# Cross attention on one core: packed Gram rows, their diagonal corrected apart, and each tile's projection finished bank by bank

## The reference

```python
text_p  = x @ W_text + b_text                 # 512 -> 512
audio_p = ctx @ W_audio + b_audio             # 384 -> 512
Q = layer_norm(text_p, g1, beta1)
K = layer_norm(audio_p, g2, beta2)
alpha = softmax(Q @ K.T / sqrt(512))          # over 77 keys
h = (alpha @ audio_p) @ W_out + b_out
out = layer_norm(h + x, g_out, beta_out)
```

## Time and profile before

| what | us |
|---|---|
| median of 3 runs | 277.99 |
| lowest and highest run | 277.51, 280.63 |
| span of the profiled execution | 275.9 |
| its own time beside the span | not listed apart; the median is 2.1 above the span |
| busy: TensorE products, VectorE, GpSimd, ScalarE | 265.3, 230.5, 203.3, 202.3 |

### The profile page before, as it was taken

One profiled execution on the slowest core, in us unless ns is written; L12 is line 12 of the kernel. 1 busy time (PEld: TensorE's weight loads), 2 busy tenths in 40 slices (PEclk: granted clock), 3 DMA queues, 4 the chain that ended last, 5 costly groups with the idle time before them and its releaser, 6 DMA issues.

```text
span 275.9 us, 5994 instructions
## 1 busy us (share of the span) xinstructions
PE 265.3 (96%) x1705; PEld 236.7 (86%) x1705; DVE 230.5 (84%) x716; ACT 202.3 (73%) x509; POOL 203.3 (74%) x223
## 2 busy tenths in 40 slices
PE   7999999999999999999999999999999999999980
PEld 6789689899999999999999999999999999999830
DVE  3767899788888888888888888888888888888895
ACT  4584392357888888888888888888888888888881
POOL 5071400114699999999999999999999999999985
PEclk9999999999999999999999999999999999999997
DMA  6818894422244444444444444444444444444116
GB/s 210 317 59 308 289 318 135 128 74 77 77 154 153 156 152 153 154 152 153 152 153 152 152 152 153 153 152 152 152 152 154 153 152 152 152 153 150 79 77 266
DMA packets 21056, 44.03 MB, mean 160 GB/s; under 512 B 2114, under 2 KB 4750, under 8 KB 21034
## 3 DMA queue, kind: packets, MB, share of 16 engines
q1 hardware_dynamic: 20410, 42.74, 45.8%
q10 hardware_dynamic: 624, 1.06, 1.2%
HBM read 21.19 MB, written 16.78 MB: 138 GB/s over the span
## 4 chain that ended last, share of the span: by engine, by line
PE 85%; DVE 5%; ACT 3%; POOL 3%; issue 1%; ACTq 1%; POOLq 0%; DVEq 0%
PE psY L1268 43%; PE psO L1280 10%; PE psT L1193 10%; PE psY L1258 7%; PE psE L1243 3%; PE psE L1244 2%; PE psY L1098 2%; PE psT L1131 1%; PE psY L1162 1%; PE psT L1162 1%; POOL zs L460 1%; POOL zs L464 1%; POOL rstd L452 1%; PE psY L1131 1%; ACTq L488 1%
## 5 line engine op out<-in xcount | busy, mean ns | idle before, releaser
L1268 PE MATMUL psY<-proj_hi,x_hi 128*128 128x464 f32 (+3 forms) x256 | 85.9, 335 | 0.0
L1268 PE MATMUL psY<-proj_hi,x_lo 128*128 128x464 f32 (+3 forms) x256 | 83.1, 325 | 0.0
L1268 PE MATMUL psY<-proj_lo,x_hi 128*128 128x464 f32 (+3 forms) x256 | 82.9, 324 | 0.0
L429 POOL TENSOR_TENSOR zs<-zs,shift 128x512 f32<-128x512 f32 x55 | 71.0, 1291 | 4.3
L423 POOL TENSOR_TENSOR zs<-zs,gain 128x512 f32<-128x512 f32 x55 | 71.0, 1291 | 1.0 <-ACT zs L616 1.0
L435 POOL TENSOR_TENSOR rstd<-stat_eps,neg_half 128x4 f32<-128x4 f32 x30 | 30.5, 1017 | 41.8 <-DVE stat_eps L921 41.8
L605 ACT ACTIVATE waste_act<-hid,sc 128x512 bf16<-128x512 f32 x60 | 43.1, 718 | 9.9 <-DVE hid L929 9.9
L1268 PEld LDWEIGHTS psY<-proj_hi,x_lo 128*128 128x128 f32 x256 | 48.4, 189 | 1.4
L1268 PEld LDWEIGHTS psY<-proj_hi,x_hi 128*128 128x128 f32 x256 | 48.6, 190 | 0.8
L1268 PEld LDWEIGHTS psY<-proj_lo,x_hi 128*128 128x128 f32 x256 | 48.6, 190 | 0.7
L574 ACT ACTIVATE x_hi<-psT 128x512 fp32r<-128x512 f32 x64 | 38.1, 596 | 13.9 <-PE psT L1193 13.9
(11 more groups left out here) (230 smaller groups left out, 487.8 us busy)
## 6 DMA issues: line engine op xcount, KB each, us to landing
xs<-in_x_dram SPq DMA_DIRECT2D x64, 256.0 KB, 3.0
out_dram<-zs SPq DMA_DIRECT2D x29, 512.0 KB, 3.9
out_dram<-zs SPq DMA_DIRECT2D x6, 256.0 KB, 2.0
xs<-in_L_xattn_W_text_dram SPq DMA_DIRECT2D x4, 256.0 KB, 3.2
xs<-in_L_xattn_W_out_dram SPq DMA_DIRECT2D x2, 512.0 KB, 5.2
wa<-in_L_xattn_W_audio_dram SPq DMA_DIRECT2D x1, 768.0 KB, 5.9
proj_hi<-proj_hi SPq DMA_DIRECT2D x1, 768.0 KB, 9.1
proj_lo<-proj_lo SPq DMA_DIRECT2D x1, 768.0 KB, 11.1
```

What stands on the lines that cost most here:

```text
L429: nc.gpsimd.tensor_tensor(zs[:, q, t, :], zs[:, q, t, :], shift[:], ALU.add).then_inc(out_ready, 1)
L1268: last = nc.tensor.matmul(psY[:, t, to:to + n0], part[:, par, t, k * P:(k + 1) * P], w[:, q, at:at + n0], start=(n == 0), stop=(n == len(P ...
```

## The change

1. **Layout.** One matrix `proj` takes the place of `proj_hi` and `proj_lo`. It has four block rows of 672 columns (ROW_W), in two halves of 336 (HALF = 80 + 256), one for each bank. The left half has 80 further columns (root, 77 low score parts, filling, low `lin`) and Gram columns 0 to 255, the right one Gram columns 256 to 511 and 80 further ones (`lin`, root, 77 high score parts, NX).
2. **Gram rows.** The high part of the doubled upper triangle stays in the upper columns; the low part is turned (transposed) and put in the free lower columns of the same rows. The blocks on the diagonal hold the halved upper triangle beside the turned low one (GpSimd, `triangle`, with `mask`; `turn`, ten transposes; ScalarE, four copies from TURNED; GpSimd adds).
3. **Exact diagonal.** The diagonal of G is found apart (`gram_square`, four squares with sums on ScalarE), nearly all of it is kept in G, and the square root of the rest (`root`, GpSimd, a power of 0.5) is a further column. `less_root` takes root times root out of each Gram row by a product over three partitions; the form adds it again, since `sc` now stands in x's row in SBUF, one column behind x.
4. **Projection.** Fourteen products a tile: `x_hi` by the left half (four of 336 columns), `x_lo` by the left Gram columns (256 and 128), then `x_hi` by the right half (four of 336), `x_lo` by the right half (three of 336, one of 208). 4288 columns. The probability transposes stand behind the first right product.
5. **The form** reads `sc` as an operand and waits for `sc_ready`, once a tile.
6. **Moves.** `t_lo(0)` and `t_hi(0)` come behind the audio work; Gram row 3 has twelve products of 128 columns; the four Gram copies of SyncE come behind the x loads of the fourth batch.

```diff
-    WIDTH = [SW + D] + [D - k * P + SW for k in range(1, KD)]
+    HALF = SW + D // 2
+    ROW_W = 2 * HALF
...
-        proj_hi = sb("proj_hi", [P, B, COLS], F32R)
-        proj_lo = sb("proj_lo", [P, B, COLS], F32R)
+        proj = sb("proj", [P, B, KD, ROW_W], F32R)
...
-        sc = sb("sc", [P, B, T, SC])
+        sc = xs_rows[:, :, :, SC_AT:SC_AT + SC]
...
 scores_and_quad:
                 nc.vector.tensor_tensor(sc[:, q, t, :], psY[:, t, at:at + SC], sc_part[:, t, :], ALU.add).then_inc(sc_ready, 1)
+                wait_if_positive(dve, sc_ready, T, i, T * (b - 1) + t + 1)
                 nc.vector.tensor_tensor_reduce(out=waste_dve[:, t, 0:QUAD_W], in0=psY[:, t, QUAD_AT:QUAD_AT + QUAD_W],
...
 project:
-                for n, (part, w) in enumerate(parts3(x_hi, x_lo, proj_hi, proj_lo)):
-                    last = nc.tensor.matmul(psY[:, t, B_AT:512], part[:, par, t, 0:P], w[:, q, 0:SW + P],
-                                            start=(n == 0), stop=(n == 2))
+                for k in range(KD):
+                    high(k, 0)
+                wait_if_positive(pe, x_lo_ready, T, i, T * (b - 1) + t + 1)
+                for k in range(2):
+                    last = nc.tensor.matmul(psY[:, t, B_AT + SW + k * P:512], x_lo[:, par, t, k * P:(k + 1) * P],
+                                            proj[:, q, k, SW + k * P:HALF], start=False, stop=(k == 1))
                 last.then_inc(projB_psum, 1)
-                for n, (part, w, k) in enumerate(PASSES):
-                    if n == passes_before and between is not None:
+                for k in range(KD):
+                    if k == before and between is not None:
                         between(b, i)
+                    high(k, 1)
+                for k in range(KD):
+                    skip = P if k == KD - 1 else 0
+                    last = nc.tensor.matmul(psY[:, t, 512 + skip:512 + HALF], x_lo[:, par, t, k * P:(k + 1) * P],
+                                            proj[:, q, k, HALF + skip:ROW_W], start=False, stop=(k == KD - 1))
                 last.then_inc(proj_psum, 1)
...
 the end:
-            project(0, END, 1, transpose_prob, 6)
+            project(0, END, 1, transpose_prob)
...
 tensor engine, preparation:
+            pe.wait_ge(root_cols_ready, 6)
+            for n, bank in ((0, ROOT_BANK[1]), (1, ROOT_BANK[0])):
+                for k in range(KD):
+                    last = nc.tensor.transpose(bank[0:3, k * P:(k + 1) * P], f32(root_cols[:, k, 3 * n:3 * n + 3]), ident[:])
+                last.then_inc(root_psum, 1)
             gram(1)
+            less_root(0)
+            less_root(1)
...
             gram(2)
-            last_gram()
+            less_root(2)
+            gram(3)
+            less_root(3)
...
             last.then_inc(kvar_psum, 1)
+            for j in range(KD):
+                turn(j)
             pe.wait_ge(g_lo, 2)
             values_product(1)
...
 GpSimd, preparation:
+            def triangle(k):
+                pool.wait_ge(g_lo, k + 1)
+                nc.gpsimd.tensor_tensor(rest[k][:, 0:P], f32(rest[k][:, 0:P]), mask[:], ALU.mult).then_inc(mask_ready, 1)
+                at = SW + k * P
+                nc.gpsimd.tensor_tensor(upper[:, k, :], f32(proj[:, 0, k, at:at + P]), mask[:], ALU.mult).then_inc(upper_ready, 1)
```

More of the change, by code:

```diff
@@ L128, in cross_attention @@
         bo_rows = sb("bo_rows", [P, H])
+        mask = sb("mask", [P, P])
+        half = sb("half", [P, KD])
+        gram_diag = sb("gram_diag", [P, KD])
+        gram_kept = sb("gram_kept", [P, KD], F32R)
+        gram_left = sb("gram_left", [P, KD])
+        root = sb("root", [P, KD])
+        root_cols = sb("root_cols", [P, KD, 6], F32R)
         cd_cols = sb("cd_cols", [P, KH, 2])
@@ L173, in cross_attention @@
         assert KH == B
+        spare_hi = x_hi[:, 1].rearrange("p t d -> p (t d)")
+        spare_lo = x_lo[:, 1].rearrange("p t d -> p (t d)")
+        rest = [spare_lo[:, 0:D], spare_lo[:, D:2 * D - P], spare_hi[:, 0:2 * P], spare_hi[:, 2 * P:3 * P]]
+        upper = spare_hi[:, 3 * P:7 * P].rearrange("p (k n) -> p k n", k=KD)
+        root_rows = x_hi[0:3, 0]
         val_a, val_b = wo_hi, wo_lo
@@ L300, in copy_gram @@
             def copy_gram(k):
-                at, n = Y_AT[k], D - k * P
-                for buf, made in ((proj_hi, g_hi), (proj_lo, g_lo)):
-                    sp.wait_ge(made, k + 1)
-                    one = f32(buf[:, 0:1, at:at + n])
-                    sp.dma_start(f32(buf[:, 1:B, at:at + n]), one.to_broadcast([P, B - 1, n])).then_inc(t_copied, 16)
+                sp.wait_ge(gram_ready, k + 1)
+                one = f32(proj[:, 0:1, k, SW:SW + D])
+                sp.dma_start(f32(proj[:, 1:B, k, SW:SW + D]), one.to_broadcast([P, B - 1, D])).then_inc(t_copied, 16)
             def body(b, i, live):
@@ L799, in _ @@
                     linear(k)
+                if k == 0:
+                    root_parts()
+            dve.wait_ge(root_psum, 1)
+            nc.vector.tensor_copy(root_rows[:, 1, :], ROOT_BANK[1][0:3, :]).then_inc(root_rows_ready, 1)
+            linear(2)
+            t_lo(0)
             t_lo(1)
-            linear(2)
             def lo_part(b, i, t):
@@ L817, in _ @@
             link(nc.vector.memset(kvar[:], 1.0))
-            last_gram_sum()
+            for k in range(2, KD):
+                t_lo(k)
             dve.wait_ge(kvar_psum, 1)
@@ L822, in _ @@
             last.then_inc(kvar_ready, 1)
-            for k in range(2, KD):
-                t_lo(k)
             linear(KD - 1)
@@ L937, in shifted_logits @@
                 for t in range(T):
-                    nc.vector.scalar_tensor_tensor(logits[:, b % 2, t, :], sc[:, q, t, 0:S], rstd[:, b, t:t + 1],
+                    nc.vector.scalar_tensor_tensor(logits[:, b % 2, t, :], sc[:, q, t, 1:1 + S], rstd[:, b, t:t + 1],
                                                    score_d[:, q, :], ALU.mult, ALU.add).then_inc(logits_ready, 1)
@@ L1033, in last_logits @@
                 dve.wait_ge(sc_ready, T * LAST + t + 1)
-                nc.vector.scalar_tensor_tensor(logits[:, LAST % 2, t, :], sc[:, q, t, 0:S], rstd[:, r, t:t + 1], score_d[:, q, :],
+                nc.vector.scalar_tensor_tensor(logits[:, LAST % 2, t, :], sc[:, q, t, 1:1 + S], rstd[:, r, t:t + 1], score_d[:, q, :],
                                                ALU.mult, ALU.add).then_inc(logits_ready, 1)
@@ L1115, in _ @@
                 last.then_inc(cxT_psum, 1)
-            def last_gram():
-                k = KD - 1
-                for h in range(KH):
-                    last = nc.tensor.matmul(W_BANK[k][:, 0:2 * P].rearrange("p (a n) -> p a n", a=2), wtT_hi[:, h, k * P:D],
-                                            wtT[:, :, h, k * P:D], start=(h == 0), stop=(h == KH - 1))
-                last.then_inc(g_psum, 1)
             def gram(k):
@@ L1154, in _, with turn @@
             gram(2)
-            last_gram()
+            less_root(2)
+            gram(3)
+            less_root(3)
+            def turn(j):
+                pe.wait_ge(mask_ready, j + 1)
+                for k in range(j + 1):
+                    last = nc.tensor.transpose(TURNED[j][:, k * P:(k + 1) * P], f32(rest[k][:, (j - k) * P:(j - k + 1) * P]), ident[:])
+                if j > 0:
+                    last.then_inc(turned_psum, 1)
             def values_product(n):
@@ L1233, in _ @@
             constant(0, C_BANK)
-            pe.wait_ge(lin_lo_ready, KD)
-            PASSES = [(a, w, k) for k in (1, 0, 2, 3) for a, w in parts3(x_hi, x_lo, proj_hi, proj_lo)]
+            pe.wait_ge(lin_lo_ready, 3)
+            pe.wait_ge(gram_ready, KD)
             def transpose_prob(b, i):
```

207 lines of the change are left out of this document (120 added, 87 removed).

## The result

| kernel | median, us | runs | lowest to highest |
|---|---|---|---|
| before, beside it | 279.31 | 4 | 277.51 to 281.94 |
| changed | 283.35 | 4 | 281.64 to 285.74 |

The ratio is 1.018, with a 95% interval of 1.013 to 1.024: the changed kernel is slower. I had forecast 278.8 with a range from 272.5 to 282.5. The same kernel, run once more beside the experiments, gave 283.25 (4 runs, 281.04 to 284.69) against 278.36 (13 runs), again 1.018 [1.009 to 1.027].

The account below looks back on a forecast made before the run. A loop of VectorE and the tensor engine waiting for each other was taken as the bound. 275.9 + 3.4 (preparation) - 2.6 (steps) - 0.4 (first) + 0.4 (last) = 276.7, plus 2.1 to the median: 278.8 us, range 272.5 to 282.5.

Parts of the forecast that it names:

- The failed step: Preparation: the root and its parts on VectorE and GpSimd were taken as hidden under the audio products, at no cost.
- The added work of the tensor engine: Preparation: the tensor engine works without a gap, so added transposes and products delay everything by 3.4 us.
- the products that take the root out: Preparation, tensor engine: four products of 512 to 128 columns, at 0.119 per 256, add 0.65 us.
- the last Gram row: Preparation, tensor engine: twelve products of 128 columns, 1.32 us, in place of four in 0.48, add 0.84 us.
- rival (c): Preparation: GpSimd's eight masked 128x128 products hold the turning if 0.87 us each or more; 281.7 or 283.3 us, chance 0.15.
- The steady step: Repeated step: a loop of VectorE and the tensor engine still bounds, falling from 6.855 to 6.77 us.
- The tensor engine's part of the loop: Steady step: fewer product columns behind the probability transposes shorten this part by 0.27 us.
- The wait in tile 1: Steady step, VectorE: the form waiting for sc costs 0.12 us in the loop, bounds nothing to 0.17.
- The second: Steady step: the other tile's wait for sc, partly covered by ScalarE's rounding, costs 0.06 us.
- The waits: Signs in steady step: VectorE below 0.4, tensor engine for parts near 0.5, GpSimd before rstd near 0.25, sc to form 0.28.
- Rival (a): Steady step: the tensor engine bounds and the step falls until GpSimd holds at 6.52; 270.9 us, chance 0.11.
- Rival (b): Steady step: the added waits on VectorE are free, so the step is 6.585; 273.0 us, chance 0.17.

Follow-up runs that it names:

- Experiment 1: Changed kernel, but GpSimd waits for the root columns before its four wo_lo subtractions: 277.87 us, ratio 1.001.
- experiment 8: Changed kernel with GpSimd's four wo_lo subtractions of 512 columns cut into eight of 256: 279.27 us, one run.
- experiment 4: Kernel before, with the probability transposes behind six products of the right bank instead of three: 281.59 us, ratio 1.011.
- experiment 5: Kernel before, with only the wait of the quadratic form for sc added: 281.82 us, one run, step 6.975.
- experiment 9: Changed kernel, but tile 0's form reads 514 columns without root part or wait; tile 1 keeps both: 280.06 us, one run, step 6.693.
- experiment 2: Changed kernel, with the form of both tiles reading 514 columns, without the root column and without the wait for sc: 280.24 us, step 6.564.
- experiment 3: Changed kernel, with the probability transposes behind the third high right product instead of the first: 277.85 us, ratio 0.999.
- experiment 6: Changed kernel, with GpSimd's wo_lo after the root columns and the probability transposes behind the third high right product: 274.79 us, ratio 0.987.
- experiment 7: Changed kernel, with GpSimd's wo_lo after the root columns and the probability transposes behind the second high right product: 273.19 us, ratio 0.979.
- 6 and 7 with less of GpSimd's work: Kernels of experiment 6 and experiment 7, with GpSimd's output shift added on 256 instead of 512 columns for each step's second tile: 273.94 and 273.41 us.

## Why the prediction was wrong

**The failed step** is the sentence of the preparation "Hidden: ... the root and its parts on VectorE and GpSimd (under the audio products)". I looked at how much work it is, six instructions on 128 x 4 numbers, and not at who runs beside it. GpSimd's `wo_lo` stands in the earlier trace rows, 6.07 us from 15.84 on, exactly there. Experiment 1 gives the columns back at 0.17 each, and experiment 8 shows that four of the six each wait out one GpSimd instruction.

The first audio product itself starts between 12.50 and 16.39 us, also in executions of kernels that do not differ up to there, as the loads come (16.39 and 15.97 have a stretch at clock 0.50 ahead of it too). So the preparation is best counted from that product (us):

| profiled execution | first audio product | from it to the root transposes | from it to the first projection |
|---|---|---|---|
| kernel before; experiments 4 and 5 | 12.50; 12.68, 12.87 | | 32.04 to 32.07 |
| changed, clock full behind the root columns (again; experiment 9) | 13.50; 12.57 | 8.99 | 39.10 |
| changed, clock 0.50 there (first profile; experiments 2 and 3) | 12.71; 13.56, 15.97 | 8.99 | 40.43 to 40.59 |
| root first (experiments 1, 6, 7, and 6 and 7 with less of GpSimd's work) | 12.87 to 16.39 | 6.22 | 36.33 to 36.35 |
| halved pieces (experiment 8) | 13.94 | 6.84 | 36.99 |

The wait for the root columns costs 39.10 - 36.35 = 2.75 us, where I had priced it at nothing, and the lower clock behind it 40.59 - 39.10 = 1.5 more in the first profile. Without the wait alone, 283.35 - 2.75 = 280.6 would have stood inside my range.

**The added work of the tensor engine** was sized low: 3.4 forecast, 36.35 - 32.07 = 4.3 measured once the wait is gone. Its terms, from the profile of experiment 7, where they stand undisturbed (the first row is of the kernel before):

```profile
12.50 4.83 PE L1098 MATMUL psY<-cxT,wa 128*128 128x308 f32 x18
...
12.99 4.83 PE L1154 MATMUL psY<-cxT,wa 128*128 128x308 f32 x18
...
20.00 2.34 PE L1179 MATMUL psY<-wtT 128*128 128x384 f32 x12
22.27 0.49 PE L1184 MATMUL psT<-x_hi 3*128 3x512 f32 x1
...
25.93 1.55 PE L1179 MATMUL psO<-wtT 128*128 128x128 f32 x12
27.41 0.32 PE L1184 MATMUL psO<-x_hi 3*128 3x128 f32 x1
...
31.18 0.55 PE L1221 MATMUL psY<-ident,x_lo 128*128 128x128 f32 x3
...
32.24 0.48 PE L1230 MATMUL psY<-wo_hi,vT_hi 128*128 128x512 f32 x1
```

The eight root transposes 0.79 (0.88 forecast), with 0.2 between the audio products and them; the products that take the root out 0.59 for the first two and 0.3 each for the others, 1.2 together (0.65), each 0.1 to 0.2 above what I took for its columns (that the change of shape costs it is a guess, not tried); the last Gram row 27.41 - 25.93 = 1.48 against 0.48, so 1.0 (0.84); the ten turns 1.06 (1.10). These add up to the 4.3 within 0.1. The 0.5 between the first two rows is not part of it: by the table, it is the loads of that execution.

**GpSimd's masked products** (rival (c)) take 0.46 each (a row of experiment 7 below), near my 0.38 and far from the 0.87 from which they decide. The turns follow the key variances without a wait. The side was right, slower, and the mechanism was not: it was GpSimd's large instructions that held VectorE, not its small ones that held the tensor engine.

```profile
24.68 0.46 POOL L428 TENSOR_TENSOR x_hi<-proj,mask 128x128 fp32r<-128x128 f32 x1
```

**The steady step.** Forecast 6.77, measured 6.69. The tensor engine's part of the loop fell as forecast: from the first product behind the transposes to the mix it is 138.44 - 137.34 = 1.10 us, where it was 152.56 - 151.18 = 1.38 (rows below and the earlier trace rows): 0.28 less, 0.27 forecast. The wait in tile 1 cost the forecast 0.12 (experiments 2 and 5). The second was put at 0.06 and is free (experiments 5 and 9): ScalarE's branch covers it in full. 6.855 - 0.27 + 0.12 = 6.705. Behind the first projection the kernel saved 4.7 us, where I had 2.6 in the steps, 0.4 in the first one and 0.4 lost at the end, so 2.6 net.

```profile
137.34 0.71 PE L1328 MATMUL psY<-proj,x_hi 128*128 128x336 f32 x3
...
138.44 0.41 PE L1358 MATMUL psO<-wo_hi,parts_t 128*128 128x512 f32 x1
```

The mix in the kernel before:

```profile
152.56 0.41 PE L1280 MATMUL psO<-wo_hi,parts_t 128*128 128x512 f32 x1
```

**The waits** came out as said: VectorE 0.3 (below 0.4), the tensor engine 0.4 (near 0.5), `rstd` 0.18 (0.25), `sc` to form 0.27 (0.28).

**Rival (a)**, the tensor engine as the bound, is false for this kernel, whose chain goes by VectorE more than by the tensor engine (the page's shares below), and true for the one with late transposes, at 6.34 of its own work, not the 6.25 that I gave it: its work fell by 6.76 - 6.34 = 0.42 a step, where I had 0.55. **Rival (b)**, waits that are free, is refuted by experiments 2 and 5. The Trainium skill, "VectorE: DVE Perf Modes", section "The DRAIN you can't avoid", says that semaphores between vector instructions cost nothing extra. Here one costs 0.12 us, because the two instructions overlap when nothing holds the second.

```profile
DVE 47%; PE 31%; issue 15%; ACT 4%; POOL 1%; ACTq 1%; DVEq 0%; POOLq 0%
```

The Trainium skill, "SBUF — State Buffer", section "🔬 SBUF: two separate sides", would have caught the failed step. VectorE and GpSimd share one pair of ports, as an exclusive lock held for the whole instruction, and the other engine blocks fully; it names VectorE's two-port modes and its instructions with two SBUF inputs. The trace agrees, in both kinds: the casts and scalings (one input) and the subtraction (two). What is 0.17 us alone is 1.2 beside 128 x 512 subtractions and 0.67 beside 128 x 256 ones.

**What stays open.** Why the changed kernel had the lower clock in half of its runs. In the first 260 us of the fourteen profiled executions the tensor engine stood idle for 1.75 us or more seven times: five times for the root columns (2.61 us), once for the load of the context (2.00, experiment 3) and once for a part of the text weights (1.75, experiment 1). The granted clock fell to 0.50 near the end of five of these seven, three of them waits for the root columns, and nowhere else in that stretch. So the idle time bears on it. But it isn't the whole cause: the clock stayed at 1.00 behind two of the five waits for the root columns, and no run moves the idle time alone. Experiment 7 shows 0.993 to 0.996 in all four runs. Experiment 6, which has no such wait either, shows 0.979 to 0.985 in three runs of ten, and the kernel before shows such runs too; none of these was profiled.

Sum against the profiled execution: 275.9 + 0.2 (first audio product later) + 4.3 (work of the tensor engine) + 2.8 (root columns) + 1.5 (lower clock) - 4.7 (steps and end) = 280.0, and 279.9 was measured. Forecast were 3.4 for the work, 2.6 for steps and end, and nothing for the others. The rest of the miss is in the median, which lies 3.4 above the profiled span, where I carried 2.1: two of its four runs have the lower mean clock.

## What to carry to other kernels

A small VectorE instruction is not small while GpSimd works through large ones: in a row of them nearly each can wait out a whole GpSimd instruction. Where an engine waits for such a row, let GpSimd start its bulk behind it, or cut the bulk in pieces; one wait on one semaphore gave back 2.75 us here, and more where the idle time would have brought the lower clock. Count a preparation from a point behind its loads, since their arrival moved it by 1.4 us between executions at full clock (12.50 to 13.94). And when a change shortens one side of a loop of two engines, look for the best place of the work between them again: here a place one product further on took the step from 6.69 to 6.545, and two further gave part of it back to a wait for a third engine.

## What the runs showed of the hardware

- VectorE's sums with two SBUF inputs are held as well, and GpSimd is slowed in turn. In experiment 7 `linear` takes 0.68 us alone and 1.54 beside `wo_lo`. Of GpSimd's subtractions, the second takes 1.73 us beside it, and the first of the changed kernel, beside the same sum, 1.81 (above); beside the small root instructions they take 1.26.

```profile
16.34 0.68 DVE L827 CUSTOM_DVE_ANT_0 waste_dve<-xs,bt_rows 128x512 bf16<-128x512 f32 x1
...
18.10 1.54 DVE L827 CUSTOM_DVE_ANT_0 waste_dve<-xs,bt_rows 128x512 bf16<-128x512 f32 x1
```

- Which of the two starts first seems to decide. L839 starts at 19.05, at the end of GpSimd's second subtraction and just ahead of the third (19.07), and takes 0.16. L840, which waits on no semaphore either, starts at 19.13, behind it, and is held to its end for 1.23.
- A wait of VectorE on its own last instruction costs 0.12 us where the two would overlap, 0.27 from start to start against 0.15.
